# A lambda layer on one core: query diagonals written by ScalarE, three plain pairs of positions instead of two, and another order in the first pair

## The reference, cut to what matters

```python
x = x + lambda_conv(group_norm(x))            # x: (32, 128, 32, 32); n = m = 1024 positions of d = 128
# inside lambda_conv, b = 32 images, k = 16, h = 4 heads, v = 32
keys    = xf @ Wk.T;   softmax_keys = softmax(keys, axis=1)
values  = bn(xf @ Wv.T, gamma_v, beta_v)      # statistics over images and v, one pair for each position m
queries = bn(xf @ Wq.T, gamma_q, beta_q)      # statistics over images, positions and heads, one pair for each k
content_lambda   = einsum('bmk,bmv->bkv', softmax_keys, values)
position_lambdas = einsum('nmk,bmv->bnkv', E, values)        # E: (1024, 1024, 16)
out = einsum('bknh,bkv->bhvn', queries, content_lambda) + einsum('bknh,bnkv->bhvn', queries, position_lambdas)
```

## Time and profile before

| | |
|---|---|
| median of 3 runs | 1473.01 us (1472.98 to 1473.51) |
| profiled execution, its own time | 1472.43 us |
| its span from the first to the last instruction | 1470.7 us |
| mean granted TensorE clock | 0.992 |
| busy: PE / PEld / DVE / ACT / POOL | 1426.4 / 1188.5 / 887.2 / 419.6 / 672.7 us |

### The profile page before, as it was taken

How to read it: one execution, slowest core, us unless ns; L and a number is a source line. 1 busy time by engine, 2 the same in 40 slices (tenths; PEclk the granted TensorE clock), 3 DMA queues, 4 the chain that set the end, 5 groups by cost and what they waited for, 6 DMA issues and landing times.

```text
span 1470.7 us, 36060 instructions
## 1 busy us (share of the span) xinstructions
PE 1426.4 (97%) x14539; PEld 1188.5 (81%) x14539; DVE 887.2 (60%) x1246; ACT 419.6 (29%) x721; POOL 672.7 (46%) x487
## 2 busy tenths in 40 slices
PE   6988799999999999999999999999999999999997
PEld 6987678888888888888888888888888888888885
DVE  7999865555555555555555555655556555555553
ACT  4774322222222222222222222222222222222220
POOL 6662454444544445443454434544355444544441
PEclk9998999999999999999999999999999999999999
DMA  8746222526234443416243343516263243425221
GB/s 288 283 169 85 60 66 57 93 64 121 64 88 69 93 93 76 93 45 121 64 104 67 78 93 90 96 37 113 64 117 68 66 91 93 93 59 91 64 57 29
DMA packets 338456, 134.62 MB, mean 92 GB/s; under 512 B 202640, under 2 KB 333824, under 8 KB 337920
## 3 DMA queue, kind: packets, MB, share of 16 engines
q1 hardware_dynamic: 338432, 134.31, 40.9%
HBM read 109.12 MB, written 25.17 MB: 91 GB/s over the span
## 4 chain that ended last, share of the span: by engine, by line
PE 93%; DVE 4%; POOL 1%; issue 1%; DMA 0%; ACT 0%; DVEq 0%; SPq 0%; POOLq 0%
PE ps_a L1109 81%; PE ps_b L1125 5%; PE ps_b L1001 4%; PE ps_a L991 2%; PE ps_a L1093 1%; DVE bn L672 1%; POOL q_diag L468 0%; DVE q_stats L697 0%; DVE v_nat L894 0%; DMA x_main<-in_x 0%; POOL s_buf L453 0%; POOL keys L428 0%; DVE pos L822 0%; DVE lam_diag L843 0%; DVE b_lo L712 0%
## 5 line engine op out<-in xcount | busy, mean ns | idle before, releaser
L1109 PE MATMUL ps_a<-v_hi,e_hi 128*128 128x512 f32 x1736 | 682.4, 393 | 6.7 <-DVE pos L822 6.7
L1109 PE MATMUL ps_a<-v_hi,e_lo 128*128 128x512 f32 x1736 | 676.9, 390 | 0.0
L1109 PEld LDWEIGHTS ps_a<-v_hi,e_hi 128*128 128x128 f32 x1736 | 326.3, 188 | 75.9 <-issue 7.1
L1109 PE MATMUL ps_a<-b_lo,e_hi 128*128 128x512 f32 x992 | 386.7, 390 | 0.0
L1109 PEld LDWEIGHTS ps_a<-v_hi,e_lo 128*128 128x128 f32 x1736 | 326.6, 188 | 65.9
L562 ACT ACTIVATE e_hi<-e_nat 128x512 fp32r<-128x512 f32 x310 | 196.2, 633 | 595.7 <-PE ps_a L1109 589.1
L468 POOL TENSOR_TENSOR q_diag<-qn,row_mask 128x1024 f32<-128x1024 f32 x128 | 253.4, 2002 | 156.2 <-PE ps_b L1125 154.9
L464 POOL TENSOR_TENSOR e_nat<-e_nat,s_buf 128x512 f32<-128x512 f32 x62 | 81.0, 1306 | 525.8 <-DVE e_lo L702 525.8
L789 DVE TENSOR_TENSOR pos<-ps_a,content 128x512 f32<-128x512 f32 x186 | 128.6, 692 | 302.3 <-PE ps_a L1109 302.3
L702 DVE TENSOR_TENSOR e_lo<-e_nat,e_hi 128x512 fp32r<-128x512 f32 x310 | 294.4, 950 | 1.6 <-ACT e_hi L562 1.2
L1109 PE MATMUL ps_a<-t_lo,e_hi 128*128 128x512 f32 x744 | 289.8, 390 | 0.0
(11 more groups left out here) (124 smaller groups left out, 869.2 us busy)
## 6 DMA issues: line engine op xcount, KB each, us to landing
e_nat<-in_L_conv_E SPq DMA_DIRECT2D x128, 512.0 KB, 4.8
res<-in_x SPq DMA_DIRECT2D x64, 256.0 KB, 6.7
out_dram<-res SPq DMA_DIRECT2D x64, 256.0 KB, 4.6
x_main<-in_x SPq DMA_DIRECT2D x24, 512.0 KB, 4.5
q_dram<-q_nat SPq DMA_DIRECT2D x4, 2048.0 KB, 7.6
q_blk<-q_dram SPq DMA_DIRECT2D x32, 256.0 KB, 5.3
x_more<-in_x SPq DMA_DIRECT2D x8, 512.0 KB, 8.6
gam_q<-in_L_conv_gamma_q SPq DMA_DIRECT2D x8, 0.1 KB, 7.8
```

Source lines behind the costliest of these rows:

```text
L1109: ins = nc.tensor.matmul(BANK_OF[i], e[:, i, j].rearrange("p n k -> p (n k)"), v[:, j], start=(STARTS[i] and j == 0 and n == 0), stop=(STO ...
```

## The change

- **Query diagonals.** `qn` and `diag` are gone. ScalarE writes `q_diag` from `q_blk` itself, in 8 instructions of 128x256 a pair, one for each position n of a tile. Scale and shift come from `q_scale_n` and `q_shift_n`, which are zero outside the block. An instruction reads 256 elements in a row and writes each of them 8 elements (32 bytes) after the last. In the loop they stand between the `split_hi` of the next pair.
- **A third plain pair.** Pairs 0, 1 and 2 are plain, 3 to 63 have seven products. The plain pairs use other slots of `e_hi` and `e_lo`.
- **First pair.** The passes are split by halves: the first two passes of the second half and the second `lambda_half` stand ahead of the third pass of the first half.
- **Value chain.** The statistics of the last group are taken for 6 images and then 2, in place of 4 and 4; a copy behind `v_shift` is gone; GpSimd's sums of keys wait for `v_affine`; `sum_keys(1)` stands ahead of `shift_keys(2)`.
- **Smaller ones.** `lam_scale` has 2 large instructions for 8 small ones; `query_moments` has 2 instructions for 16 aggregations; `e_sums` of the first seven-product pair stands ahead of `queries_rstd`.

```diff
-        FIRST_SLOTS = ((0, 1, 2, 3), (0, 1, 4, 5))
+        FIRST_SLOTS = ((0, 1, 2, 3), (4, 5, 6, 0), (1, 2, 3, 4))
...
-            def diag(t, slot):
-                pool.wait_ge(qn_ready, t + 1)
-                pool.tensor_tensor(q_diag[:, slot].rearrange("p (q n) -> p q n", n=TN),
-                                   qn[:, slot].unsqueeze(2).to_broadcast([P, BH, TN]),
-                                   row_mask[:].unsqueeze(1).to_broadcast([P, BH, TN]),
-                                   ALU.mult).then_inc(q_diag_ready, 1)
...
             shift_keys(1)
+            sum_keys(1)
             shift_keys(2)
             values_rstd()
-            sum_keys(1)
-            pool.memset(lam_diag[:], 0.0).then_inc(lam_zeroed, 1)
+            pool.wait_ge(v_affine, 1)
             sum_keys(2)
             sum_keys(3)
+            pool.wait_ge(content_ready, 1)
+            e_sums(PLAIN, PLAIN % 2, 64, first=True)
             queries_rstd()
...
+            def norm_queries(p, i, part):
+                if part.start == 0:
+                    if i % 2 == 0:
+                        act.wait_ge(q_blk_loaded[i // 2], (p // PPB) * 16 + 16)
                     if not (isinstance(p, int) and p == 0):
-                        act.wait_ge(q_diag_ready, p * 2 - 1 + t)
-                    norm_q(p * 2 + t, t, (i % 4) * 2 + t)
+                        act.wait_ge(queried, p)
+                of = q_blk[:, (i % 4) * 2:(i % 4) * 2 + 2].rearrange("p t f -> p (t f)")
+                to = q_diag[:].rearrange("p t (f n) -> p n (t f)", n=TN)
+                for n in part:
+                    ins = nc.scalar.activation(to[:, n], of, ACT.Identity, bias=q_shift_n[:, n:n + 1], scale=q_scale_n[:, n:n + 1])
+                if part.stop == TN:
+                    ins.then_inc(q_diag_ready, 1)
...
+            PARTS = (range(0, 2), range(2, 4), range(4, 5), range(5, 6), range(6, 7), range(7, 8))
...
                     for n in range(NP - 1):
                         split_hi(p + 1, n, (i + 1) % 2)
-
+                        norm_queries(p, i, PARTS[n])
...
             lambda_half(0)
+            pe.wait_ge(e_lo_ready, NP)
+            for j in range(MJ, J):
+                pe.wait_ge(v_hi_ready, j + 1)
+                plain_sums(0, j, (0, 1))
             lambda_half(1)
             sum_lambdas()
             pe.wait_ge(v_lo_ready, 2)
             for j in range(MJ):
                 ins = plain_sums(0, j, (2,))
             ins.then_inc(half_done, 1)
-            pe.wait_ge(e_lo_ready, NP)
-            for j in range(MJ, J):
-                pe.wait_ge(v_hi_ready, j + 1)
-                plain_sums(0, j, (0, 1))
-            spread_content()
             pe.wait_ge(v_lo_ready, 4)
             for j in range(MJ, J):
+                if j == J - 2:
+                    spread_content()
                 plain_sums(0, j, (2,), last=(j == J - 1))
...
+            plain_pair(1, average_queries)
+            plain_pair(2, lambda: query(1))
...
-            pair(2, first=True)
-            with pe.Fori(3, PAIRS) as p:
+            pair(PLAIN, first=True)
+            with pe.Fori(PLAIN + 1, PAIRS) as p:
                 pair(p)
```

More of the change, by code:

```diff
@@ L411, in _ @@
             pool.memset(ones_sq[:], 1.0).then_inc(ones_ready, 1)
+            pool.memset(lam_diag[:], 0.0).then_inc(lam_zeroed, 1)
             def norm_images(k):
@@ L635, in _ @@
             t_hi(2, 2)
+            first_hi(2, 3)
             act.wait_ge(q_affine, 1)
-            norm_queries(0, 0)
-            act.wait_ge(half_done, 2)
+            norm_queries(0, 0, ALL)
+            norm_queries(1, 1, ALL)
+            for n in range(3):
+                split_hi(PLAIN, n, PLAIN % 2)
             t_hi(3, 4)
             t_hi(5, 3)
-            norm_queries(1, 1)
-            for n in range(NP - 1):
-                split_hi(2, n, 0)
-            for i in range(2, PPB):
+            norm_queries(2, 2, ALL)
+            for n in range(3, NP - 1):
+                split_hi(PLAIN, n, PLAIN % 2)
+            for i in range(PLAIN, PPB):
                 pair(i, i, False)
@@ L776, in _ @@
             some_query_stats(1, range(10, KD)).then_inc(q_stats_done, 1)
-            value_stats(A - 1, A - 1, range(GB))
             keys_top(2)
@@ L838, in lam_scale @@
                 link(nc.vector.reciprocal(inv_sum[:], sum_ps))
+                masks = row_mask[:].rearrange("p (h a) -> p h a", a=A)
+                for half in range(2):
+                    rows = slice(half * HALF, (half + 1) * HALF)
+                    ins = nc.vector.tensor_tensor(inv_mask[rows], inv_sum[rows].unsqueeze(2).to_broadcast([HALF, B // TN, A]),
+                                                  masks[rows, half].unsqueeze(1).to_broadcast([HALF, B // TN, A]), ALU.mult)
+                link(ins)
@@ L839, in lam_scale @@
                 dve.wait_ge(lam_zeroed, 1)
[L840 to L841 removed]
+                for half in range(2):
                     rows = slice(half * HALF, (half + 1) * HALF)
[L843 to L847 removed]
+                    nc.vector.tensor_tensor(
+                        lam_diag[rows].rearrange("p (s h a v) -> p h s a v", h=2, a=A, v=V)[:, half],
+                        ps_b[rows].rearrange("p i (s f) -> p (i s) f", s=2)[:, :, 0:P].rearrange("p s (a v) -> p s a v", v=V),
+                        inv_mask[rows].unsqueeze(3).to_broadcast([HALF, B // TN, A, V]), ALU.mult).then_inc(lam_masked, G // 2)
@@ L918, in _ @@
                 value_split_lo(i)
+            lam_scale()
             for n in range(4):
@@ L959, in pair @@
                     split_lo(p + 1, 5, (i + 1) % 2)
-            for i in range(2, PPB):
-                pair(i, i, i == 2, False)
+            for i in range(PLAIN, PPB):
+                pair(i, i, i == PLAIN, False)
             with dve.Fori(1, BLOCKS - 1) as blk:
```

206 lines of the change are left out of this document (100 added, 106 removed).

## The result

The changed kernel took 1464.38 us (median of 5 runs, 1463.49 to 1466.31), the kernel before 1472.98 us (median of 5, 1472.0 to 1473.51): a ratio of 0.9949, with a 95% interval of 0.9937 to 0.996. The forecast was 1464.1 us in a range of 1460.8 to 1468.0, so the time lies inside it, 0.3 us from the forecast. The profiled execution took 1464.14 us, its span is 1462.2 us and its mean granted clock 0.994.

A forecast was written before the change was run, and what follows sets the result against it. TensorE was taken as the bound, its loop staying at 20.50 us a pair. Gains ahead of the loop sum to 8.9 us: span 1470.7 to 1461.8, own time 1463.5, plus 0.58 for the median: 1464.1 us, range 1460.8 to 1468.0.

The forecast's parts named there:

- the marker: Start of pair 3's second product on TensorE, forecast at 204.2 us against 213.06 before.
- a diagonal at 0.75 us or more: ScalarE's diagonals: forecast at about 0.59 us each; this duration or more would show the prediction wrong.
- the breaking point: ScalarE in the loop: it fills the 20.50 us pair when a diagonal costs 2.1 us; chance 0.04.
- I take nothing: ScalarE's strided write of the diagonals: no added cost, 0.586 us for 256 elements, eight in 4.04 us.
- The estimate of 0.8 us: Strided write at one more access each: 0.8 us an instruction, 2.4 us more ahead of the first query.
- Rival 2: ScalarE's strided write costs 0.16 us or more each, lengthening the wait at `query(0)`: 1465.4 to 1466.5 us; chance 0.18.
- rival 3: Value chain starts later: contention before `v_var` is not given back, 1.5 us, 1465.6 us; chance 0.12.
- The 1.6 us to be given back: Value chain: `v_scale` without GpSimd's sums beside it and the dropped copy give back about 1.6 us.
- Forecast 3.5 us: First pair: pair 1 starts at 149.8 in place of 153.35 us, with about 0.7 us of waits left.
- `head` behind `e_lo` number 6: VectorE in pair 3: `head` stands behind `e_lo` 3 to 6 and ends at 204.2 us, delaying the second product.
- the 8.9 us: Whole gain ahead of the loop: start of pair 3's second product at 204.2 against 213.06 us.
- No lower clock after 120 us: TensorE: a sign of being right, with no idle of over 3 us and no lower clock after 120 us.

The follow-up runs named there:

- The cut in eighths: The changed kernel with each diagonal written by eight instructions of 128x32, 64 a pair in place of 8; 1703.27 us, one run.
- the power first: The changed kernel with the queries' power ahead of the three sums of E in GpSimd's queue; 1467.26 us, ratio 0.9956.
- E early: The changed kernel with the load of E for pair 2 issued ahead of the loads of `res`; 1464.31 us, ratio 0.994.

## Why the prediction was right, and where it was not

The time came out right because the loop kept its period and the order of events ahead of it was the one forecast. That it came out within 0.3 us is luck: the marker is 1.1 us late, and 0.7 of that is taken back behind it by scatter. And one of the prediction's own signs of being wrong, a diagonal at 0.75 us or more, was met.

- **The loop.** Right: 20.467 us a pair (20.468 before), with ScalarE's time of waiting for TensorE as the cover (932.5 us of it before, 564.7 now). The cut in eighths shows what happens past the breaking point.
- **The diagonal's duration.** The term "I take nothing" for the strided write failed: 0.87 us and not 0.586, eight in a row 5.19 us and not 4.04. For a single instruction the nearest row, VectorE's reduction at 0.64 ns an element, was too low as well: it is 0.28/256 = 1.1 ns. For eight in a row it was nearly right, 0.66 us each and 1.3 more against 5.19/8 = 0.65 us and 1.15 more, since 0.25 us of each instruction is covered by the one before, where 0.09 was taken. The estimate of 0.8 us, with 2.4 more for eight, was twice too high. Two arguments for "nothing" were none. That `norm_q` "still lies on 0.836 ns an element" is so by construction, since its 479 ns are one of the two points from which the 0.836 was worked out; and it reads runs of 4 elements, while here single elements are written. Rival 2 held in the duration, and its price in the end did not show, for the diagonals began 1.0 us before the forecast.
- **The value chain.** Forecast as nothing gained, and the spread came 1.2 us late, so this is rival 3 in part. Some 0.5 us of it is a late start: `key_top`, at 97.84 us before, is at 98.35. The rest is the `e_lo` that meet GpSimd's addition. They were scaled, 4.07 by two thirds, to 2.8, and took 3.46. Three alone take 1.90 and two 1.29 (both are rows of the changed kernel), so meeting that addition costs 2.17 us in either case, a sum to be added and not a rate. The Trainium skill, SBUF — State Buffer, "SBUF: two separate sides", has it as a lock that one of the two engines holds for its whole instruction, and the rows agree: one `e_lo` of the two lasts 2.81 us and the other 0.72. The 1.6 us to be given back behind the variance were right against the kernel before, 5.71 us from the start of the power to the spread (107.98 to 113.69) and now 4.20 (110.80 to 115.00). But the old chain in the changed kernel needs only 4.94 (108.48 to 113.42), so of the new chain's own merit 0.7 is left, and that doesn't pay for a variance 2.3 us later (110.55 against 108.23).
- **The first pair.** Forecast 3.5 us, measured 2.7 (153.35 to 150.65): the mechanism is right, and the waits are 0.74 and 0.28 in place of 0.4 and 0.3. TensorE itself had made up for the late chain, since its clock rose sooner than before (0.99 and not 0.88 from 118 to 124 us) and two passes took 8.7 us (115.42 to 124.16) in place of 10.0. What was late was VectorE, with the low parts at 144.4 us in place of 143.8. The old order of passes costs 1.6 us at pair 1.
- **Pair 1 and `query(0)`.** The order was right: `res`, E for pair 2, E for pair 3, GpSimd's sums, diagonals, query. E for pair 3 came at 160.3 us and not 161.5. GpSimd's queue did not delay the power, as the prediction had it: GpSimd stood idle for 0.28 us until VectorE asked for it. What made the scale late was contention, 1.6 us on two tiny instructions of VectorE ahead of the power (0.66 and 1.22 us, above). The two errors, diagonals 1.15 us longer and started 1.0 us earlier, cancel: 171.50 against 171.2. That is luck. The wait is shorter than forecast, 1.02 and not 1.8 us, because TensorE itself came 1.1 us later.
- **Pairs 2 and 3.** The 6.68 us and the lower clock behind it are gone, as forecast, and the wait that takes their place, `head` behind `e_lo` number 6, was in the sum at 1.8 us and measures 1.92. The marker is 1.1 us late, 0.65 of it at pair 3's first product (199.15 against 198.5) and 0.4 behind that. But the 8.9 us were not the third plain pair's merit: by the single parts undone, it is 1.1 us, the passes 1.6, the diagonals 4.8, the value chain -1.1 (medians), 6.4 of 8.6. Only the diagonals' share is beyond the scatter of medians, and a lower clock behind a short wait sits in some of these runs. The parts overlap at one wait, so they need not add up.
- **The clock.** "No lower clock after 120 us" holds for the profiled execution. It does not hold for each. Eight profiles have a wait of 1.8 to 1.9 us ahead of pair 3's second product: in six the 84 matmuls behind it take 19.3 us, in two (the old passes and the power first) 20.9. The changed kernel's two longer runs have a mean granted clock of 0.993 and its three shorter ones of 0.994 or 0.995, which fits. No profile of it in a longer run exists, so for that kernel this is argued and not shown.
- **The end.** 0.7 us of the gain stands behind the last query and was in no term. Span less marker is 1256.2, 1256.9, 1257.2 and 1257.6 us in four kernels in which TensorE has the same work there (diagonals on GpSimd, changed, E early, before), so it is scatter.
